# Issuing the residual's load three steps later on ScalarE in a fused gated cross-attention and mixing block

## The reference

```
x = x + tanh(g_xattn) * attn(layernorm(x), ctx)
    attn: 16 heads of 32; q, k, v = relu(...); softmax(q k' / sqrt(32)) v; relu(o W' + b)
x = x + tanh(g_ffn) * mix(layernorm(x))
    mix:  xr, xk = mu * x + (1 - mu) * x_prev   (x_prev: the token before)
          sigmoid(xr W_r) * (relu(xk W_k)^2 W_v)
```

## Time and profile before

| | |
|---|---|
| median of 3 runs | 2981.95 us (2980.19 to 2983.81) |
| profiled execution, its time | 2980.25 us |
| its span | 2978.4 us, 71298 instructions |
| busy: PE, DVE, ACT, POOL | 96%, 78%, 53%, 35% |
| granted TensorE clock, mean | 0.993 |
| DMA | 408.56 MB, mean 137 GB/s |

### The profile page before, as it was taken

How to read it: one execution, slowest core, us unless ns; L and a number is a source line. 1 busy time by engine, 2 the same in 40 slices (tenths; PEclk the granted TensorE clock), 3 DMA queues, 4 the chain that set the end, 5 groups by cost and what they waited for, 6 DMA issues and landing times.

```text
span 2978.4 us, 71298 instructions
## 1 busy us (share of the span) xinstructions
PE 2860.3 (96%) x23168; PEld 2190.6 (74%) x23168; DVE 2330.1 (78%) x4175; ACT 1564.3 (53%) x2828; POOL 1045.4 (35%) x902
## 2 busy tenths in 40 slices
PE   3899999999999999999999999999999999999998
PEld 2677777777777777777777777777777777777776
DVE  5777877878878878878877877877878778788774
ACT  4445555555455455555555555555555555554552
POOL 0233333333343343333333333333333333333434
PEclk9899999999999999999999999999999999999999
DMA  5544445445445445445445445455455454454431
GB/s 168 150 122 140 144 124 155 140 127 155 135 131 156 137 131 154 133 137 150 131 142 149 128 143 153 120 149 152 120 152 146 124 152 142 124 156 137 130 109 41
DMA packets 405258, 408.56 MB, mean 137 GB/s; under 512 B 164577, under 2 KB 329441, under 8 KB 405218
## 3 DMA queue, kind: packets, MB, share of 16 engines
q1 hardware_dynamic: 352994, 340.92, 39.6%
q10 hardware_dynamic: 52224, 67.12, 7.3%
HBM read 272.64 MB, written 134.22 MB: 137 GB/s over the span
## 4 chain that ended last, share of the span: by engine, by line
PE 59%; DVE 16%; DMA 10%; SPq 7%; issue 5%; ACT 1%; ACTq 1%; DVEq 0%; POOL 0%; POOLq 0%
PE bank L951 29%; DMA out_dram<-x 8%; PE bank L918 7%; PE bank L932 6%; PE bank L906 5%; PE bank L944 4%; DVE m_nat L699 4%; DVE o_val L718 4%; SPq L272 3%; DVE st L652 3%; DVE k_raw L682 2%; PE bank L893 2%; PE bank L875 2%; SPq L258 2%; SPq L270 2%
## 5 line engine op out<-in xcount | busy, mean ns | idle before, releaser
L496 ACT ACTIVATE probs<-bank 128x512 f32<-128x512 f32 x1024 | 596.4, 594 | 455.7 <-PE bank L918 228.1
L699 DVE TENSOR_REDUCE m_nat<-bank 128x2 fp32r<-128x512 f32 x1024 | 695.4, 685 | 107.4 <-PE bank L906 106.7
L477 ACT ACTIVATE q_st<-bank 96x512 fp32r<-96x512 f32 x512 | 304.1, 594 | 718.9 <-PE bank L875 718.8
L918 PE MATMUL bank<-q_st,k_st 97*128 97x256 f32 x2048 | 449.9, 301 | 64.2 <-ACT probs L496 47.4
L718 DVE RECIPROCAL o_val<-bank 128x256 f32<-128x256 f32 x256 | 449.1, 1754 | 56.1 <-PE bank L944 51.7
L918 PEld LDWEIGHTS bank<-q_st,k_st 97*128 97x128 f32 x2048 | 341.8, 191 | 153.8 <-issue 58.5
L906 PE MATMUL bank<-k_st,q_st 96*128 96x256 f32 x2048 | 431.6, 293 | 7.4 <-DMA k_st<-k_dram 4.8
L397 POOL TENSOR_TENSOR xm<-xm 128x512 f32<-128x512 f32 x128 | 133.3, 1041 | 787.2 <-ACT xm L540 787.2
L906 PEld LDWEIGHTS bank<-k_st,q_st 96*128 96x128 f32 x2048 | 358.2, 192 | 59.8 <-issue 6.2
L708 DVE CAST m_t<-bank 4x256 fp32r<-4x256 f32 x256 | 105.1, 411 | 285.5 <-PE bank L884 285.4
L364 POOL TENSOR_TENSOR o_lo<-o_mv,o_hi 128x512 fp32r<-128x512 f32 x128 | 164.8, 1287 | 430.0 <-ACT o_hi L503 430.0
(11 more groups left out here) (90 smaller groups left out, 6026.6 us busy)
## 6 DMA issues: line engine op xcount, KB each, us to landing
k_st<-k_dram SPq DMA_DIRECT2D x256, 256.0 KB, 3.6
k_raw<-ctx_t_dram SPq DMA_DIRECT2D x256, 128.0 KB, 3.0
x_ln<-x_dram SPq DMA_DIRECT2D x256, 128.0 KB
k_dram<-k_high SPq DMA_DIRECT2D x64, 512.0 KB, 3.0
k_dram<-k_raw SPq DMA_DIRECT2D x64, 512.0 KB, 4.5
k_st<-k_dram SPq DMA_DIRECT2D x256, 128.0 KB, 3.5
o_dram<-o_val SPq DMA_DIRECT2D x256, 128.0 KB, 1.7
o_mv<-o_dram SPq DMA_DIRECT2D x512, 64.0 KB, 2.2
```

Source lines behind the costliest of these rows:

```text
L477: nc.scalar.activation(q_st[0:QK, c, :, P * u:P * u + P], tp_bank[0:QK, :].rearrange("p (g t) -> p g t", g=GR), ACT.Copy).then_inc(q_stack ...
L496: nc.scalar.activation(probs[:, n // GR % 2, n % GR, :, :].rearrange("p v t -> p (v t)"), st_bank[n % 2][:, :], ACT.Exp, scale=SCALE).then ...
L699: nc.vector.tensor_reduce(m_nat[:, c % 2, :, n % GR:n % GR + 1], s_bank[n % 2][:, :].rearrange("p (u y) -> p u y", u=NU), AX_X, ALU.max, n ...
L918: mm = nc.tensor.matmul(st_bank[n % 2][:, T * v:T * v + T], k_st[0:ST, c, g, P * v:P * v + P], q_st[0:ST, c, g, :], start=True, stop=True)
```

## The change

In ScalarE's list the call of `load_x1(i - 1, 1 - par)` moves from behind `exponent(i, 1)` and `q_stack(i, 3, 0)` to behind `exponent(i, 4)`. The load, its wait and its tile stay as they are.

```
                 exponent(i, 1)
                 split_high(i, 0)
                 q_stack(i, 3, 0)
-                load_x1(i - 1, 1 - par)
 
                 exponent(i, 2)
...
                 exponent(i, 3)
 
                 exponent(i, 4)
+                load_x1(i - 1, 1 - par)
                 kt_relu(i - 2, 1)
                 q_high(i + 1, 1)
                 o_high(i - 1, 1)
```

## The result

The changed kernel took 2934.94 us (median of 4 runs, 2933.22 to 2936.94); the kernel before, beside it, 2981.07 us. The ratio is 0.9846, with a 95% interval of 0.9829 to 0.9863. The forecast was 2920 us with a range of 2908 to 2952.

What follows compares the result with a forecast made beforehand. PE, busy 96% of the span, was taken to bound the kernel. Removing its stall gains 66 us, o_high behind the load gives back 4, so 2981.95 - 62 = 2920 us, range 2908 to 2952.

Steps and rivals of the forecast that it cites:

- its own signs of being wrong: Wrong if L918's wait for m_t, L951's for o_lo or o_hi's for o_mv exceeds some 20 us, among other signs.
- Removed from step 1: ScalarE's wait for the store before exponent(i,2) goes, ending PE's stall at shifted score 4: 1.10 us a turn, 66 us.
- (a): PE's idle time shown before shifted score 4, waiting for the exponent: 0.79 us a turn.
- (b): Idle time at PE's stall hidden because the row counts from the previous matmul's modelled end: 0.16 us more a turn.
- (c): PE's restart: the L918 pair after the stall takes 0.40 us instead of 0.25, so 0.15 us a turn.
- m_t, costed at nothing: Before shifted score 4, the 4 KB transfer behind the store lands before PE needs it; bounds nothing to the whole gain.
- The wait in step 4, costed at nothing: Behind exponent(i,4), the wait for the store is over about 1 us before ScalarE comes to it.
- The transfer, hidden: x, issued 1 us later, lands with more than 4 us left before its only reader, add_x(i-1,0): costs nothing.
- o_high behind the load: 4 us: In step 4 o_high waits for o_mv, making o_lo late for project(i-1,1): 0.2 us in 16 to 20 turns; bounds 0 to 18.
- o_mv "would come sooner": In issue order, x's 512 KB would come after o_mv's first parts instead of just ahead of it; no separate size given.
- The rival at 0.10: o_mv becomes the wait in every turn: 66 - 18 = 48 us gained, 2934 us; chance 0.10.
- The slower rival: At o_high(i-1,1), x meets o_mv in the DMA queues: 1.7 us later, net 0.8 us a turn, 3030 us; chance 0.04.

Runs made afterwards that it cites:

- The run with the short store: Kernel before the change, load of x still in step 1, but the store writes only 64 of the 512 columns; 2916.88 us, ratio 0.9789.
- the run with the small load in step 1: Kernel before the change, load of x still in step 1 but bringing only 64 of the 512 columns; 2977.39 us, ratio 0.9994.

## Why the direction was right and one term far too small

By its own signs of being wrong the prediction failed, though the time fell in its range: ScalarE's wait for o_mv and PE's wait for o_lo are both above 20 us (170.3 and 33.7).

- *Removed from step 1.* Right in mechanism: all 60 waits are gone. The price of 1.10 us was low: 1.34 us was measured. Terms (a) and (b) together, 0.95 us by my rows, were 0.87. Term (c), the restart, was 0.15 and measured 0.46. By the starts it is 0.20 us in the pair behind the stall, 0.11 between L960 and the matmul after it, and 0.14 around the next shifted score: I had priced the pair alone. In the pile-up behind the stall the exponents are done late, and PE's weight load waits for them (43.8 us in 87 times, 4.1 in 10 in the changed kernel). The run with the short store shows this part with hardly any idle time.
- *m_t, costed at nothing.* Right: 18.1 us in 4 waits, 16.7 before, all in the first 120 us. The Trainium skill (DMA: Bandwidth & Descriptors, Queues, rings and completion order) says that descriptors are taken in ring order on each DMA engine, so m_t stands behind the store's share where they use the same one. No delay of PE from this shows in a middle turn of the changed kernel.
- *The wait in step 4, costed at nothing.* Right: the row is gone.
- *The transfer, hidden.* Right for its own reader: x is issued at 1512.68, lands in 4.4 us (median) and add_x starts at 1523.43.
- *o_high behind the load: 4 us. This is the step that failed.* It measured 0.71 us a turn, some 41 us, more than twice its upper bound of 18. It took 0.2 us in 16 to 20 turns, because the rows showed ScalarE idle for o_mv in 16 turns only and I put the start of o_high in the others down to ScalarE's pile-up. In the trace before, o_high starts within 0.2 us of o_mv's last landing in every one of turns 6 to 61, within 0.05 us in 38: pile-up and landing ended together (at 7.34 and 7.40 us after shifted score 3, medians, the first from the run with the small load in step 1), and without the pile o_high could come no sooner. Counted from shifted score 3 (means over these turns), o_lo was done at 9.50 us; PE without a stall is ready for it at 9.38, as the run with the load behind o_high shows, and starts 0.15 us after o_lo is done, which I had left out. So 0.27 us a turn was lost with o_lo no later than before, in all turns and not in 16; 0.24 of it because PE came 1.34 us earlier, not 1.10.
- *o_mv "would come sooner".* It came later, and this is the rest of the same step. o_mv's last landing moved by 0.2 us (5.60 for 5.38 us, medians). All of x landed before it in each of these turns, by 0.42 us in the median. Issued 0.8 us behind o_mv's first part, x delays the last part more than issued 0.2 us ahead (5.60 against 5.16 us with the load at the end of step 2), and with no x beside it o_mv takes 3.33: the two are on different queues, and being in flight together counts for more than the order. In the kernel before a third transfer, load_v (L459), went beside o_mv too, issued 0.86 us behind it and landing at 4.91; in the changed kernel it has landed by 1.10. I had said that nothing is won by that. Later landing gives 0.19 us of the loss, the longer passes on GpSimd 0.16, and 0.09 stands behind the wait: with the 0.27, the 0.71 us.
- *Sum.* Over 57 turns the removal was worth 14 us more than I said (0.24 us each), the first three stalls some 7 us more again (10 us by turn 6, for 3 x 1.10), and what was given back was 37 us more than my 4: 16 us too much gain in all, for the 15 by which the forecast missed. Two errors of opposite sign brought it this near. The rival at 0.10 named the right wait, but its agreement to 1 us is luck: it had 66 - 18, and the runs show about 86 - 41. Against it I had noted "less is ahead of it", which was the wrong test. The slower rival's price (o_mv later by 1.7 us) was wrong for the same reason: o_mv was already slowed by all of x in the kernel before.

The Trainium skill, in the same section, says that each DMA engine takes turns between the queues that have work for it. The three sizes of x agree with this: o_mv takes 3.52, 4.85 and 5.60 us with 64, 256 and 512 columns of x beside it on the other queue. Whether the length of the rows plays a part (x in 2 KB rows, o_mv in 256 B) wasn't tried.

## What to carry to other kernels

When a stall is taken away, list every transfer that the stalled engine needs in the next few microseconds and ask how much slack each had with the stall's own length taken off: here o_lo was done 1.3 us before PE's first matmul on it (median; 0.9 in the turn shown), which starts at the soonest 0.15 us after it, and the stall was worth 1.34. A load that nobody waits for can still be dear; place it where no transfer that somebody does wait for is in flight, and don't count on the order of issue across two queues to keep them apart. Look too at what the pass behind a late transfer runs beside: here a start 0.01 us later cost GpSimd 0.8 us. And follow each instruction behind a moved wait, not only the kind that was stalled before.

## What the runs showed that I had not expected

- The time is not monotone in the place of the load: 2981, 2957, 2918, 2935, 2895 and 2898 us going down ScalarE's list. From the end of step 2 to behind exponent(i,4), 1 us later in issue, it is 17 us in the wrong direction.
- o_low's pass on GpSimd and L674 on DVE lengthen each other: 1.28 and 1.59 us when GpSimd starts first by a little, 2.06 and 0.67 us when it starts 0.01 us later.
- A late release costs PE more than its idle time: at idle times of 3.0 us in the whole span (short store) the two stretches behind shifted score 4 were still 0.35 us a turn longer. The idle row of the kernel before said 47.4 us, the whole price was near 80 (1.34 us in 60 turns).
- 448 of 512 KB less to store shortened the store's time to landing by 1 us only, from 4.1 to 3.1.
